# Cross-attention of a decoder layer with its scores turned: context blocks in partitions, 512 tokens in columns

## The reference

```python
x = x + attn(layernorm(x))                # 16 heads of 32, window: |i-j| <= 16 and i-j even
x = x + xattn(layernorm(x), ctx, ctx)     # one head of 512 over 2048 context rows a batch element
x = x + ffn(layernorm(x))                 # silu(x wg) * (x wu), then wd; 1536 hidden

def xattn(query_source, key_source, value_source):
    q, k, v = query_source @ Wq + bq, key_source @ Wk + bk, value_source @ Wv + bv
    attn = softmax(einsum('bqd,bkd->bqk', q, k))
    return einsum('bqk,bkd->bqd', attn, v)
```

## Time and profile before

| | us |
|---|---|
| median of 3 runs (1216.16 to 1216.86) | 1216.77 |
| the profiled execution | 1214.97 |
| its span | 1212.8 |
| TensorE busy | 1178.3 (97%) |
| VectorE busy | 746.7 (62%) |
| ScalarE busy | 494.9 (41%) |
| GpSimd busy | 418.8 (35%) |

### The profile page before, as it was taken

The page is one execution under the profiler, slowest core; times in us unless marked ns, Lnnn a source line. Parts: engine busy times, 40 slices in busy tenths (PEclk is TensorE's granted clock), DMA queues, the critical chain, the costliest instruction groups (busy, mean ns, idle before and its releaser), DMA issues.

```text
span 1212.8 us, 17589 instructions
## 1 busy us (share of the span) xinstructions
PE 1178.3 (97%) x6672; PEld 956.6 (79%) x6672; DVE 746.7 (62%) x1268; ACT 494.9 (41%) x854; POOL 418.8 (35%) x382
## 2 busy tenths in 40 slices
PE   6999999999999999999999999999999998999998
PEld 4877777777767888888778888877888887888886
DVE  6667675684686642333563422346899877788875
ACT  5354454454364532222542222236444344444431
POOL 1255765764764010000000100042545742444431
PEclk9999999999999999999999999999999999999999
DMA  8010110201046440000442010021511111511101
GB/s 286 10 36 9 37 62 1 79 36 37 35 140 200 150 154 27 27 26 26 152 127 96 27 35 26 17 79 54 198 53 53 52 53 52 174 53 53 53 18 70
DMA packets 50188, 87.03 MB, mean 72 GB/s; under 512 B 4544, under 2 KB 16832, under 8 KB 50112
## 3 DMA queue, kind: packets, MB, share of 16 engines
q1 hardware_dynamic: 50112, 86.00, 21.5%
HBM read 69.21 MB, written 16.78 MB: 71 GB/s over the span
## 4 chain that ended last, share of the span: by engine, by line
PE 83%; DVE 6%; ACT 4%; POOL 4%; issue 3%; DMA 0%; ACTq 0%; POOLq 0%; DVEq 0%
PE work L175 15%; PE work L177 14%; PE work L176 14%; PE score L177 5%; PE score L175 5%; PE score L176 5%; PE score L2370 4%; PE score L2372 3%; PE score L2371 3%; PE score L1125 2%; PE work L2370 2%; PE work L2372 2%; PE work L2371 2%; PE work L1669 2%; PE score L1139 1%
## 5 line engine op out<-in xcount | busy, mean ns | idle before, releaser
L1549 DVE TENSOR_TENSOR pt_l<-work,pt_h 128x512 fp32r<-128x512 f32 x64 | 44.0, 690 | 168.8 <-ACT pt_h L1474 168.8
L1447 POOL TENSOR_TENSOR xr<-xr,bv_row 128x512 f32<-128x512 f32 x16 | 22.0, 1374 | 333.1 <-DMA xr<-x_scratch 333.1
L2036 POOL TENSOR_TENSOR hid<-fg,hid 128x512 fp32r<-128x512 f32 x48 | 84.8, 1787 | 105.2 <-ACT hid L2100 105.2
L497 POOL TENSOR_TENSOR probs<-probs,band 128x544 f32<-128x544 f32 (+1 forms) x64 | 89.5, 1399 | 78.2 <-ACT probs L628 77.9
L1474 ACT CAST pt_h<-work 128x512 fp32r<-128x512 f32 x64 | 37.3, 587 | 173.1 <-PE work L1669 173.0
L175 PE MATMUL score<-ct_h,x_q_h 128*128 128x512 f32 x256 | 102.8, 401 | 1.6 <-DVE ct_l L1543 1.0
L175 PE MATMUL work<-cn,pt_h 128*128 128x512 f32 x256 | 101.8, 398 | 0.0
L177 PE MATMUL score<-ct_h,x_q_l 128*128 128x512 f32 x256 | 100.1, 391 | 0.0
L177 PE MATMUL work<-cn,pt_l 128*128 128x512 f32 x256 | 99.9, 390 | 0.0
L175 PE MATMUL work<-wqkv_h,xt_h 128*128 128x512 f32 (+1 forms) x256 | 94.9, 371 | 5.2 <-DVE xt_l L804 5.2
L176 PE MATMUL score<-ct_l,x_q_h 128*128 128x512 f32 x256 | 99.9, 390 | 0.0
(11 more groups left out here) (243 smaller groups left out, 3025.5 us busy)
## 6 DMA issues: line engine op xcount, KB each, us to landing
x_stage<-in_ctx_t SPq DMA_DIRECT2D x16, 512.0 KB, 4.4
x_stage<-in_ctx_n SPq DMA_DIRECT2D x16, 512.0 KB, 4.8
w_stage<-in_wg_t SPq DMA_DIRECT2D x12, 512.0 KB, 3.7
w_stage<-in_wu_t SPq DMA_DIRECT2D x12, 512.0 KB, 3.7
wd_raw<-in_wd_t SPq DMA_DIRECT2D x12, 512.0 KB, 3.6
x_in<-in_x SPq DMA_DIRECT2D x16, 256.0 KB, 2.7
xs<-in_x SPq DMA_DIRECT2D x4, 1024.0 KB, 5.6
x_scratch<-xs SPq DMA_DIRECT2D x4, 1024.0 KB, 4.4
```

The source lines that it names most:

```text
L497: PL.tensor_tensor(probs[:, n % 2, :, 0:w], probs[:, n % 2, :, 0:w], band[:, c0:c0 + w].unsqueeze(1).to_broadcast([P, HPG, w]), ALU.mult). ...
L1549: V.tensor_tensor(pt_l[:, 4 * c:4 * c + 4, :], src.rearrange("p (k q) -> p k q", q=P), pt_h[:, 4 * c:4 * c + 4, :].bitcast(F32), ALU.subtr ...
L2036: PL.tensor_tensor(hid[:, q, 1, :], g[:, q, :], hid[:, q, 0, :].bitcast(F32), ALU.subtract).then_inc(hidl_done, 1)
```

## The change

Cross-attention now goes through 4 groups of 512 tokens. For each group it goes through 16 blocks of 128 context rows; one block of one group is called a slice here, j = 0 to 63.

- Scores of a slice have 128 context rows in partitions and 512 tokens in columns: 12 matmuls, with the context stationary. ACT copies them from PSUM into a ring of 20 slices in SBUF (`x_s`, 18 slices ahead of their use), and DVE keeps a running maximum over the group's blocks (`x_maxima`).
- For each group, TensorE transposes the maxima (4 transposes, L1798), DVE reduces them and makes the shift, and spreads it; 4 matmuls of plain f32 with the identity (L1806) bring the shift to all partitions, and ACT copies it (`x_shifts`).
- For each slice DVE adds the shift (`dve_sub`), ACT takes the exponential and casts the high part, DVE subtracts for the low part. The result is already turned as the weighted sum needs it: no transposes. 12 matmuls of 512 columns add the slice into the four banks of `score`, which hold the output turned.
- POOL adds up the exponentials over slices (`x_acc`); 4 matmuls with a column of ones (L1819) sum over partitions once for each group.
- The group's output is cast and split (`act_out`, `dve_out`) and projected in 4 blocks of 12 matmuls (at `RESULT_AT`), and `dve_result` scales by the inverse sums and adds the residual.
- Context, both ways round, is no longer kept: for every group all 16 pieces of both are read from DRAM and split again, through two buffers each (`load_ct`, `load_cn`, `act_ct`, `dve_ct`, `act_cn`, `dve_cn`).
- There is no loop: all 64 slices are written out. The feed-forward network's first work is spread over slices 31 to 61. Five of its seven transposes stand at slices 52, 54, 57, 60 and 61, two behind them.
- At the end of self-attention, the first 18 score slices take the place of the first two tiles' scores and the first tile's transposes.

```diff
+LEAD = 18
+SRING = 20
+TURN_AT = {NS * CK - CK + 4: 0, NS * CK - CK + 6: 1, NS * CK - CK + 9: 2, NS * CK - CK + 12: 3, NS * CK - CK + 13: 4}
...
+    def load_ct(sp, n):
+        if n >= 2:
+            sp.wait_ge(ct_lo, n - 1)
+        sp.dma_start(ct_raw[:, n % 2].rearrange("p k c -> p (k c)"), ctx_t[n // NP // (NS // NB), n % NP])\
+            .then_inc(ct_landed[n % 2], 16)
...
+    CN_AT = {cn_slot(m): m for m in range(1, NPIECES)}
+    CT_AT = {2 * n - LEAD - 2: n for n in range(LEAD // 2 + 1, NPIECES)}
+    RESULT_AT = {CK * (g + 1) + 1 + t: ST * g + t for g in range(NS - 1) for t in range(ST)}
...
+    def pool_sum(pool, j):
...
+            nc.gpsimd.tensor_tensor(acc[:], acc[:], pr[:, j % 2, :], ALU.add).then_inc(acc_done, 1)
...
+    def act_cn(act, m):
+        act.wait_ge(cn_landed[m % 2], 16 * (m // 2) + 16)
+        if m >= 2:
+            act.wait_ge(block_done, 2 * m - 2)
+        A.copy(cn_h[:, m % 2], cn_raw[:, m % 2]).then_inc(cn_hi, 1)
...
+    def act_scores(act, j):
+        act.wait_ge(sc_ready, j + 1)
+        A.copy(s_at(j), s_bank(j)).then_inc(sc_copied, 1)
...
+    def act_probs(act, j):
+        act.wait_ge(sub_done, j + 1)
+        if j >= 2:
+            act.wait_ge(acc_done, accs(j - 2))
+            act.wait_ge(ptl_done, j - 1)
+        A.activation(pr[:, j % 2, :], s_at(j), ACT.Exp).then_inc(e_done, 1)
+        act.wait_ge(e_done, j + 1)
+        if j >= 2:
+            act.wait_ge(block_done, j - 1)
+        A.copy(pt_h[:, j % 2, :], pr[:, j % 2, :]).then_inc(pth_done, 1)
...
+    def dve_sub(dve, j):
+        dve.wait_ge(mb_copied, j // CK + 1)
+        V.tensor_tensor(s_at(j), s_at(j), shifts[j // CK % 2][:], ALU.add).then_inc(sub_done, 1)
...
+    def dve_probs(dve, j):
+        dve.wait_ge(pth_done, j + 1)
+        V.tensor_tensor(pt_l[:, j % 2, :], pr[:, j % 2, :], pt_h[:, j % 2, :].bitcast(F32), ALU.subtract)\
+            .then_inc(ptl_done, 1)
...
+    def pe_program(pe):
+        for j in range(NSL):
+            g, i = j // CK, j % CK
+            if j + LEAD < NSL:
+                pe_scores(pe, j + LEAD)
+            if j and not i:
+                pe_sums(pe, g - 1)
+            if i == CK - 2 and g + 1 < NS:
+                pe_maxima(pe, g + 1)
+            if i == CK - 1 and g + 1 < NS:
+                pe_shift(pe, g + 1)
+            if j in RESULT_AT:
+                pe_project(pe, RESULT_AT[j])
+            pe_weighted(pe, j)
+            if j in TURN_AT:
+                if TURN_AT[j] == 0:
+                    pe.wait_ge(sc_copied, NSL)
+                ffn.pe_turn(pe, TURN_AT[j])
```

More of the change, by code:

```diff
@@ L1476, in act_exps @@
-    def act_exps(act, g, par):
-        act.wait_ge(shift_done, g + 1)
-        if not starts(g):
-            act.wait_ge(pt_ready, g * 4)
-            act.wait_ge(sum_done, g)
-        for c in range(SB):
-            nc.scalar.activation(pr[:, 512 * c:512 * c + 512], score[:, c, :], ACT.Exp,
-                                 bias=shift[:, par:par + 1], accum_out=sums[:, c:c + 1]).then_inc(e_done, 1)
-    def act_finish(act, g):
-        act.wait_ge(tr_ready, g + 1)
-        nc.scalar.copy(ot_h[:], work[:, 3, :]).then_inc(oth_done, 1)
@@ new lines, in pe_shift, with pe_sums @@
+    def pe_shift(pe, g):
+        out = ring.take(pe, ("mb",)) if not g else work[:, 3, :]
+        pe.wait_ge(spread_done, g + 1)
+        for t in range(ST):
+            last = PE.matmul(out[:, P * t:P * t + P], spread[:, t, :], ident[:], start=True, stop=True)
+        last.then_inc(mb_ready, 1)
+    def pe_sums(pe, g):
+        pe.wait_ge(acc_done, (CK - 1) * (g + 1))
+        if not g:
+            pe.wait_ge(one_done, 1)
+        if g + 1 < NS:
+            pe.wait_ge(mb_copied, g + 2)
+        else:
+            pe.wait_ge(rinv_done, g)
+        for t in range(ST):
+            last = PE.matmul(work[:, 3, t:t + 1], acc[:, P * t:P * t + P], one[:], start=True, stop=True)
+        last.then_inc(rs_ready, 1)
@@ new lines, in pe_weighted @@
+    def pe_weighted(pe, j):
+        g, i, m = j // CK, j % CK, j // 2
+        if j % 2 == 0:
+            pe.wait_ge(cn_lo, m + 1)
+        pe.wait_ge(ptl_done, j + 1)
+        for d in range(DK):
+            if not j:
+                if d == 0:
+                    pe.wait_ge(exp_done, NS * UN)
+                if d == 2:
+                    pe.wait_ge(o_copied, 2 * NS * HG)
+            elif not i:
+                pe.wait_ge(otl_done, DK * (g - 1) + d + 1)
+            c = slice(P * d, P * d + P)
+            last = three(PE, score[:, d, :], cn_h[:, m % 2, j % 2, c], cn_l[:, m % 2, j % 2, c],
+                         pt_h[:, j % 2, :], pt_l[:, j % 2, :], i == 0, i == CK - 1)
+            if i == CK - 1 and d < DK - 1:
+                last.then_inc(o_ready, 1)
+        last.then_inc(block_done, 1)
@@ new lines, in pe_project @@
+    def pe_project(pe, n):
+        g, t = n // ST, n % ST
+        pe.wait_ge(otl_done, DK * g + DK)
+        if not n:
+            pe.wait_ge(wv_lo, 2)
+            ring.wait_last(pe, 2)
+        elif n <= (NS - 1) * ST:
+            pe.wait_ge(x2_done, n)
+        elif t == 1:
+            pe.wait_ge(rinv_done, NS)
+        else:
+            pe.wait_ge(x2_done, n - 1)
+        c = slice(P * t, P * t + P)
+        for d in range(DK):
+            last = three(PE, y_bank(n), ot_h[:, d, c], ot_l[:, d, c], wv_h[:, d, :], wv_l[:, d, :],
+                         d == 0, d == DK - 1)
+        last.then_inc(y_ready, 1)
```

1272 lines of the change are left out of this document (665 added, 607 removed).

## The result

| | before | after |
|---|---|---|
| median, us | 1216.77 | 1224.33 (5 runs, 1222.68 to 1226.43) |
| the profiled execution, us | 1214.97 | 1222.68 |
| waits of TensorE in the late slices, 46 to 63 | | 22.5 |
| slow matmuls behind them | | 9.9 |
| the same two at the exit | 0.9 + 0.9 | 9.0 + 2.1 |

The changed kernel is slower: its time is 1.0071 of before's, 95% interval 1.0053 to 1.0088. I had forecast 1200 with 0.78 on faster. The two kinds of loss in the table are read from the starts of TensorE's matmuls. A start that comes over 0.3 us later than the matmul before it needs is a wait; one that is late by 0.02 to 0.3 us is a slow matmul. Of the 9.9 us in the late slices about 8 are matmuls of 512 columns 0.43 apart instead of 0.227 and short ones at the same half speed; most of the rest is the first distance behind a wait, 0.31.

A forecast was written before the change was run, and what follows sets the result against it. Cross-attention was taken as bound by TensorE's instruction count: -37.4 - 4.5 + 9.5 + 1 + 11.5 + 2.5 + 1 = -16.4, from 1214.97 to 1198.6 us profiled, median 1200; range 1192 to 1210, for 8 in 10 1188 to 1219.

The forecast's parts named there:

- Transposes removed: Cross-attention on TensorE: 16 tiles by 5 groups of four transposes at 0.468 us go, 37.4 us saved.
- new groups: Added TensorE work, four times: transposes 0.47, column sums 0.9, shift matmuls 1.0; 9.5 us in all, bounds 7 and 13.
- slices 0 to 45: Cross-attention's earlier slices: 5.44 us each, other engines mostly covered; about 1 us lost, bounds 0 and 5.
- Rival 3: Slices 0 to 45: sharing with POOL makes VectorE the bound and the kernel slower, 1236 us; chance 0.12.
- Late slices, 11.5: Slices 46 to 63: no scores left, so the DVE and ACT chain holds TensorE; 11.5 us lost, from 2 to 20.
- The one for the last shift, 2.2: In front of slice 47's matmuls: TensorE waits some 2.2 us for DVE's last shift, made behind slice 47's low part.
- Pace of slices 53 to 63, 5.8: Last 11 slices: the chain makes a pair take 6.4 to 6.5 us instead of 5.44; 5.8 us lost.
- a rate of 0.53: Cross-attention: beside POOL, DVE operations with both inputs in SBUF go at 0.53 of their speed.
- Exit, 1: First feed-forward iteration: four results and two transposes in place of one each; 1 us lost, bounds 0 and 3.
- its 4.5: Waits at batch element edges and before the feed-forward network, with late starts, go away; 4.5 us saved.
- Entry, 2.5: Last attention group before cross-attention: ACT's two query casts and a late shift on DVE; 2.5 us lost, bounds 0 and 5.
- Rival 2: Group ends, entry and exit: waits at their upper bounds give the gain back, 1217 us, no change; chance 0.12.

The follow-up runs named there:

- e1: Changed kernel with POOL's running sum of exponentials replaced by one constant fill per group (softmax not normalised): 1217.0 us, 1.0004 of before.
- e5: Changed kernel with 66 unused matmuls (15.0 us) put before TensorE's waits in slices 47, 50, 54, 56 and 59: 1219.6 us, 1.0025 of before.
- e6: Changed kernel with ACT's casts and DVE's low parts of the feed-forward transposes one slice later in their programs: 1218.7 us, 1.0015 of before.
- e9: Separate small kernel running DVE and POOL operations alone, then together; no kernel time, DVE's row with both operands in SBUF ended 0.54 us after POOL's.
- e10: e8 and e1 together, all six orders and no running sum on POOL: 1196.7 us, 0.9837 of before.
- e4: Changed kernel with POOL's last two residual additions (tiles 14 and 15) behind the first feed-forward weight sums at the exit: 1218.0 us, 1.0016 of before.
- e2: Changed kernel with DVE's shift of a slice made one slice earlier, ahead of the previous slice's low part: 1216.4 us, 1.0007 of before.
- e3: Changed kernel with POOL's four feed-forward token sums moved from slices 46 to 49 to slices 48 to 51: 1222.5 us, 1.0048 of before.
- e7: Changed kernel with POOL's residual before its sum, and DVE's result before the low part in slices 49 to 52: 1222.4 us, 1.0049 of before.
- e8: Changed kernel with e2, e3, e4, e6, e7 and the group's shift chain before the low part in slices 14, 30, 46: 1199.5 us, 0.9855 of before.
- e11: e8 with the second weight set's casts and low parts at slices 50 to 52 and the exit's second result earlier: 1196.7 us, 0.9840 of before.

## Why the prediction was wrong

By its steps, in us of the profiled execution; it forecast 1198.6 and got 1222.7, 24.1 more.

- **Transposes removed, new groups, slices 0 to 45: right.** In the middle there is no idle time, and slices without a projection start 5.44 apart (570.28, 575.72, 581.16). The weighted sums of slices 16 and 32 start at 537.49 and 637.75, 100.3 us apart, as the forecast's 87 + 10.9 + 2.4. The three groups cost 2.26 each time, 9.0 in all instead of 9.5. Slices 0 to 45 have no wait over 0.3 us and 0.5 of slow matmuls, against the 1 of the forecast. Rival 3 is refuted: sharing with POOL does cost DVE there (181 us busy in 250, and 163 in e1 without the sum), and it stays covered.
- **Late slices, 11.5: the step that failed.** They lost 32.4, 20.9 more. The waits of slices 46 to 48 were 7.8 against 4.1, those of 49 to 52 were 5.0 against 0, those of 53 to 63 were 9.7 against 5.8 + 1.6, and the slow matmuls 9.9 against 0. So nearly half of the miss is slow matmuls, a term that I put at nothing without a reason: TensorE's clock behind its waits, about 8 of the 9.9 us, which e5 took away. The waits were mis-sized for these reasons. The one for the last shift, 2.2, was 6.0, because I put POOL's token sums nowhere. Slices 49 to 52, which "lose nothing", had a wait of 4.6: the result stands behind a low part and behind POOL's bias. The transposes, at 0.4 each for their own time in the chain, cost 2.2 to 2.4 in three slices, because what stands behind `fxt` on DVE waits for TensorE and ACT too (e6); part of those waits is the pace of the chain, the next term.
- **Pace of slices 53 to 63, 5.8 (within the 11.5): the chain right, the mechanism and price of the sharing wrong.** I made POOL's share a rate of 0.53 from one row of 2.31 us. It is exclusion (e9), so a low part beside `x_acc` lasts 1.2 to 1.5, not 1.0. The Trainium skill (SBUF — State Buffer, SBUF: two separate sides) says so outright: the pair of ports is an exclusive lock, held for a whole instruction, and not a split of bandwidth. The runs agree (2.86 us beside 2.34); I had drawn on a page that only speaks of contention. With the orders right this is what is left: without the sum the late slices lose 5.0 less (e10).
- **Exit, 1: mis-sized by about 9.** It lost 11.1. In before it was 1.8, of which 0.9 is the wait of 0.78 that the forecast had already taken off with its 4.5. I counted DVE's and TensorE's fullness. What held was POOL's order, with two transfers ahead of weight sums (e4).
- **Entry, 2.5: about nothing.** From 335 us to the first weighted sum (448.24) the waits over 0.3 us are 6.9; in before, from 335 to 450, they are 6.9 too, and the slow matmuls differ by 0.1. One wait of 4.1 at 345, behind ACT's two query casts (1.99 us at 347.08), stands in place of one of 1.8. But the wait in front of 390, which I said would stay, is gone, and so is one of 1.2 in front of 375. Why was not tried.

20.9 + 9.2 for the exit - 2.4 for the entry is 27.7, 3.6 more than the miss. The groups (0.5) and slices 0 to 45 (0.5) came out lower than forecast. Self-attention's waits and slow matmuls before 340 us are 0.4 less than in before, and what the execution spends beside its span is 1.8 instead of 2.2. The other 1.8 I have not settled; single executions of this kernel lie as far apart.

Rival 2, the gain given back at the switches, comes nearest with 1217, but not by its own places: it allowed 20 for slices 46 to 48, which had 7.8 of waits, and the clock was not in it either. What decided was not one large mechanism but several orders (e2, e3, e4, e6, e7), in most of which an instruction that waits for another engine stands in front of one that needn't, and the clock behind the waits. e8 and e11 change the orders and get about the forecast's time, so the sum of the work was right and the sum of the waits was not.

## What to carry to other kernels

When a chain between engines has no slack, list for each engine in order what stands ahead of the critical instruction and what that itself waits for; price the wait, not the instruction's length. Look at the granted clock behind each wait of TensorE, and charge a long wait with the slow matmuls that follow: here 9.9 us beside 22.5. Keep long GpSimd operations away from stretches where VectorE works from SBUF on the critical path, or give VectorE's operation an operand in PSUM.

## What the runs showed of the hardware

- VectorE operations that read both operands from SBUF, and copies within SBUF, exclude GpSimd's additions by whole instructions, and the other way round. In e9 a VectorE row with both operands in SBUF ended 0.54 us after GpSimd's, at 512 and at 1024 columns (1.72 and 2.86 us instead of 0.69); an SBUF copy took 2.56 instead of 0.43, four columns 2.31 instead of 0.16. In the kernel itself, e3 brought a copy from 2.45 to 0.43 by moving GpSimd's work away. GpSimd in turn grew from 1.26 to 1.70 each (two rows at 28.42 take 3.37). The operation with one operand in PSUM and the reduction from PSUM stayed at 0.69 and 0.68.
- After a wait of 5.8 us TensorE ran its next six matmuls of 512 columns 0.43 to 0.57 us apart, 1.2 GHz, and then 0.23 again; behind one of 0.94 us (739.54) it did not. Among waits of 2.0 to 2.3 us, three were followed by eight matmuls at half speed each (776.72, 786.98, 800.14) and the one at the exit (840.43) by none, so the length of a wait alone does not decide it. Matmuls of no use in the waits kept the granted clock at 1.00 and made the kernel 4.7 us faster.
